# Dense identity products on TensorE ahead of twelve fronts and between the scores of the first heads' fill, with scores two steps less ahead

## The reference

```python
s0A: q = x @ W_q; latent = (x @ W_k + x @ W_v) @ W_down_kv       # attention with decay
     scores = (q_h @ k_h.T) / sqrt(d) * exp(-0.01 * |t - t'|)    # 16 heads of 16
     out = softmax(scores) @ v_h, heads joined, @ W_o
s1M, s3M: out = sum over experts of gate * gelu(x[top_k] @ w1) @ w2   # 8 experts, expert choice
s2B: retention: scan over time of v, times q, layernorm, gate, @ Wo
s4C: attention with rotary q and k, mask of blocks, window and 4 global keys
s5F, s7F: out = gelu(x @ U1 @ V1) @ U2 @ V2                      # low rank, 1024 hidden
s6D: gated recurrence: short convolutions, scan, rms norm, gate, @ Wo
```

## Time and profile before

| | |
|---|---|
| median of 3 runs | 3270.99 us (3268.53 to 3271.0) |
| profiled execution | 3270.93 us, span 3269.2 us |
| mean granted clock of TensorE | 0.914 of full speed |
| TensorE (PE) busy | 2802.9 us, 86% |
| VectorE (DVE), ScalarE (ACT), GpSimd (POOL) busy | 60%, 48%, 31% |

### The profile page before, as it was taken

How to read it: one execution, slowest core, us unless ns; L and a number is a source line. 1 busy time by engine, 2 the same in 40 slices (tenths; PEclk the granted TensorE clock), 3 DMA queues, 4 the chain that set the end, 5 groups by cost and what they waited for, 6 DMA issues and landing times. The chain is left out here.

```text
span 3269.2 us, 48231 instructions
## 1 busy us (share of the span) xinstructions
PE 2802.9 (86%) x15883; PEld 1690.3 (52%) x15883; DVE 1958.6 (60%) x4266; ACT 1558.7 (48%) x2949; POOL 1004.0 (31%) x1384
## 2 busy tenths in 40 slices
PE   6599999999986299997883499996969997888879
PEld 3244444444443198985551498983534443534443
DVE  6578878888826744443558644444956663527852
ACT  3347777777751145453111345442326665245544
POOL 3322222222201145452001245442664442120112
PEclk9779999999998599998996699997979998898879
DMA  7813232323224144432003244423243442200001
GB/s 254 282 46 83 66 86 67 85 67 80 62 70 134 45 91 86 95 71 65 0 0 130 65 96 84 98 38 89 79 123 96 101 99 66 56 1 0 0 7 46
DMA packets 183271, 253.89 MB, mean 78 GB/s; under 512 B 39416, under 2 KB 124152, under 8 KB 183056
## 3 DMA queue, kind: packets, MB, share of 16 engines
q1 hardware_dynamic: 151616, 216.89, 22.3%
q0 software_dynamic: 30720, 33.98, 6.5%
q10 hardware_dynamic: 720, 0.33, 0.1%
HBM read 156.53 MB, written 93.00 MB: 76 GB/s over the span
## 5 line engine op out<-in xcount | busy, mean ns | idle before, releaser
L2000 DVE CUSTOM_DVE_ANT_0 s0Ah_SD<-s0Ah_ps_s,s0Ah_table 128x1024 f32<-128x1024 f32 x512 | 607.1, 1223 | 157.1 <-PE s0Ah_ps_s L2055 157.1
L2024 ACT ACTIVATE s0Ah_PM<-s0Ah_ps_x 128x512 f32<-128x512 f32 x1024 | 530.1, 601 | 188.0 <-PE s0Ah_ps_x L2080 98.1
L2055 PE MATMUL s0Ah_ps_s<-s0Ah_plus_k,s0Ah_plus_q 48*128 48x512 f32 x1024 | 422.9, 477 | 31.9 <-DMA s0Ah_minus_k<-s0Ah_ones 28.0
L1980 POOL TENSOR_TENSOR s0Ah_DG<-s0Ah_SD,s0Ah_mx 128x128 f32<-128x128 f32 x512 | 205.5, 401 | 554.0 <-DVE s0Ah_mx L2000 554.0
L2055 PEld LDWEIGHTS s0Ah_ps_s<-s0Ah_plus_k,s0Ah_plus_q 48*128 48x128 f32 x1024 | 167.4, 193 | 279.6 <-DVE s0Ah_mx L2000 176.7
L2100 PE MATMUL s0Ah_ps_v<-s0Ah_PM,s0A_V 128*17 128x512 f32 x2048 | 271.9, 603 | 0.0
L2080 PE MATMUL s0Ah_ps_x<-s0Ah_plus_q,s0Ah_plus_k 50*128 50x512 f32 (+3 forms) x640 | 238.0, 389 | 0.0
L2260 DVE CUSTOM_DVE_ANT_0 s4Ch_SD<-s4Ch_ps_s,s4Ch_table 128x264 f32<-128x264 f32 x448 | 177.4, 431 | 94.6 <-PE s4Ch_ps_s L2345 90.1
L2080 PE MATMUL s0Ah_ps_x<-s0Ah_minus_q,s0Ah_minus_k 50*128 50x512 f32 (+3 forms) x640 | 218.9, 390 | 0.0
L2289 ACT ACTIVATE s4Ch_PM<-s4Ch_ps_x 128x512 f32<-128x512 f32 (+1 forms) x256 | 131.4, 564 | 113.7 <-PE s4Ch_ps_x L2372 110.5
L2089 PE MATMUL s0Ah_ps_x<-top_ident,s0Ah_DG 128*128 128x128 f32 x512 | 169.0, 330 | 0.0
(11 more groups left out here) (438 smaller groups left out, 6736.3 us busy)
## 6 DMA issues: line engine op xcount, KB each, us to landing
s0A_parts<-s0Ap_sp_top SPq DMA_DIRECT2D x32, 512.0 KB
s0A_parts<-s0Ap_sp_rest SPq DMA_DIRECT2D x32, 512.0 KB
s1W_raw_w<-in_L_ffn_w SPq DMA_DIRECT2D x16, 1024.0 KB
s3W_raw_w<-in_L_ffn_w SPq DMA_DIRECT2D x16, 1024.0 KB
s0Ah_plus_q<-s0A_parts SPq DMA_DIRECT2D x64, 128.0 KB, 2.5
s0Ah_plus_k<-s0A_parts SPq DMA_DIRECT2D x64, 128.0 KB, 3.0
s0Ah_minus_q<-s0A_parts SPq DMA_DIRECT2D x64, 128.0 KB, 3.0
s0Ah_minus_k<-s0A_parts SPq DMA_DIRECT2D x64, 128.0 KB, 3.2
```

The lines of the kernel that those rows point to most:

```text
L1980: nc.gpsimd.tensor_tensor(DG[p % 3][:, r * TB + t, :], SD[i % NSD][:, t * P:(t + 1) * P], mx[p % 3][:, r * TB + t:r * TB + t + 1].to_broad ...
L2000: nc.vector.tensor_tensor_reduce(SD[i % NSD][:, :], ps_s[i % 2][:, :, :].rearrange("p a n -> p (a n)"), table[:, (TB - 1 - t) * P:(TB - 1 ...
L2024: nc.scalar.activation(PM[n % NPB][:, :], ps_x[u % NX][:, :], ACT.Exp).then_inc(e_ok, 1)
L2055: x = nc.tensor.matmul(ps_s[i % 2][:, half, :], q[at(r), t * P:(t + 1) * P], k[at(r), half * GT:(half + 1) * GT], start=True, stop=True)
```

## The change

A new helper issues n matmuls of the identity (128 x 128) with the identity repeated four times (128 x 512) into a bank. It waits for nothing, signals nothing, and nobody reads its results; the bank is one whose first real use comes later on the same engine.

It is called first in TensorE's program of eight functions: `low_rank_ffn` (5 products), `retention` (7), `gated_recurrence` (5), `route` (6), `experts` (8, ahead of the first transposes), `project_rotary` (5), `heads_window` (6) and `project_heads` (8). As `low_rank_ffn`, `route`, `experts` and `project_heads` run twice, that makes 77 products in twelve phases. In the fill of `heads_decay` one product follows each score step from 19 on (9 products). AHEAD goes from U + 14 to U + 12, and TURN with it from 12 to 10.

```diff
@@ -155,6 +155,14 @@
             turn(b * 2 + h, h, True, True)
     turn(NG - 2, 0, True, False)
     turn(NG - 1, 1, False, False)
+
+
+def keep_dense(nc, ident, bank, n):
+
+
+    for _ in range(n):
+        nc.tensor.matmul(bank, ident[:, :], ident[:, :].unsqueeze(1).to_broadcast([P, GT // P, P]),
+                         start=True, stop=True)
 
 
 class FfnWeights:
@@ -382,6 +390,7 @@
                     at = (2 * k + j) * P
                     x = nc.tensor.matmul(ps_o[:, j * D:(j + 1) * D], QT[:, at:at + P], v2[:, :], start=True, stop=True)
                 x.then_inc(o_mm, 1)
+            keep_dense(nc, ident, ps_o[:, :], 5)
             pe.wait_ge(W.weights, W.loaded)
             turned(0, 0)
             turned(0, 1)
@@ -573,6 +582,7 @@
 
         @block.tensor
         def _(pe):
+            keep_dense(nc, ident, ps_m[:, :], 7)
             pe.wait_ge(raw.next_in, 16 * 4)
             pe.wait_ge(consts, START + 1)
 
@@ -817,6 +827,7 @@
 
         @block.tensor
         def _(pe):
+            keep_dense(nc, ident, ps_i[:, 0, :], 5)
             pe.wait_ge(W.weights, W.loaded)
             pe.wait_ge(consts, START + 1)
 
@@ -1059,6 +1070,7 @@
 
         @block.tensor
         def _(pe):
+            keep_dense(nc, ident, ps_p[:, :], 6)
             pe.wait_ge(weights, 48)
             def score(g):
                 pe.wait_ge(ln.hTok, START + (g + 1) * DC)
@@ -1343,6 +1355,7 @@
                                                      stop=(m == M - 1 and k % 2 == 1 and n == 2))
                             if m == M - 1 and k % 2:
                                 x.then_inc(o_mm, 1)
+            keep_dense(nc, ident, ps_o[:, 0, :], 8)
             transposes(0, 0, 0)
             expert_turns(pe, turn)
 
@@ -1833,6 +1846,7 @@
 
         @block.tensor
         def _(pe):
+            keep_dense(nc, ident, ps_r[:, 0, :], 5)
             ln.tensor(pe, 0)
             pe.wait_ge(raw.next_in, 16 * 3)
             pe.wait_ge(consts, START + 2)
@@ -1864,7 +1878,7 @@
 
     NP = B * H // 2
     U = 2 * TB
-    AHEAD = U + 14
+    AHEAD = U + 12
     TURN = AHEAD - U - 2
     NPB, NSD, NX = 12, 3, 3
     plus = [[ph.sb(f"plus_{n}{i}", [P, T], F32R) for n in "qk"] for i in range(4)]
@@ -2106,6 +2120,8 @@
                     score(i, half)
                 if i == U + 2:
                     turned(0)
+                if i > U + 2:
+                    keep_dense(nc, ident, ps_x[NX - 1][:, :], 1)
             for i in range(N):
                 ahead = i + AHEAD
                 if (i + TURN) % U == 0 and (i + TURN) // U < NP:
@@ -2413,6 +2429,7 @@
                 if t == TB - 1:
                     x.then_inc(pv_mm, 1)
 
+            keep_dense(nc, ident, ps_x[0][:, :], 6)
             pe.wait_ge(sign_ok, START + 1)
             for m in range(3):
                 x = nc.tensor.transpose(ps_x[NX - 1][:, m * P:(m + 1) * P], signs[:, m, :], ident[:, :])
@@ -2531,6 +2548,7 @@
 
         @block.tensor
         def _(pe):
+            keep_dense(nc, ident, ps_o[0][:, :, :].rearrange("p a n -> p (a n)"), 8)
             pe.wait_ge(weights, 16 * 2 * DC)
             pe.wait_ge(pick_ok, START + NG * DC)
             pe.wait_ge(top_ok, START + 1)
```

## The result

The changed kernel takes 3279.8 us (median of 20 executions, 3264.6 to 3284.4) against 3271.0 before (20 executions, 3266.5 to 3274.4). The ratio is 1.002, with a 95% interval of 1.0011 to 1.0029: about 0.2% slower, where the prediction said 3254.5 us and a range of 3245 to 3263.5. The 20 executions stand in two groups, nine from 3264.6 to 3274.9 and eleven from 3279.5 to 3284.4. The profiled execution (3271.4 us, span 3269.6) is of the lower group, so what its profile shows stands for that group and not for the median.

What follows compares the result with a forecast made beforehand. VectorE bounds the heads' fill, TensorE the steady loop, which starts at half clock. Heads -6.4, project_heads -3.4, experts -3.2, FFNs -2.4, rotary -0.7, route -0.4 sum to -16.5 us: 3270.93 to 3254.5, range 3245 to 3263.5.

Steps and rivals of the forecast that it cites:

- The failed step: Heads' fill: clock rises 4.4 us after 175.9, at 180.3; two steps cold, seven warm, fill ends at 190.6.
- -8.4 + 1.8 + 0.2 = -6.4 us: Heads: steady loop at full clock from its start -8.4, longer fill +1.8, two more steps carrying scores at loop's end +0.2.
- third rival: Heads' fill: its products do not raise the clock, loop begins cold; +12.3 us in place of -6.4, total 3273; chance 0.07.
- first rival: Fronts: the clock holds everywhere, so fronts taken at half give all; 3246 us or a little less; chance 0.10.
- TURN: Heads' steady loop: turned maxima of each later pair move from step 4 to 6; cost 0, 2 us to spare.
- fourth rival: Heads' steady loop: maxima come late, TensorE stands at 31 pair starts, 1 us each, total 3285; chance 0.04.
- The fronts: Waits ahead of stages: project_heads -3.4 us, experts -3.2, FFNs -2.4, rotary -0.7, route -0.4; window heads, retention, recurrence 0.
- second rival: Fronts: clock falls behind transposes; FFNs and route 0, experts -0.95 each, rotary +1; -9.3 us in all, 3261.6; chance 0.15.

Runs made afterwards that it cites:

- e3_ahead28: Kernel before with only AHEAD = U + 12 and TURN 10, no products anywhere: 3271.9 us, ratio 0.9999.
- e1_fronts: Changed kernel without its products in the heads' fill, AHEAD back at U + 14, products in the twelve fronts: 3259.9 us, ratio 0.9963.
- e4_burst4: e1_fronts plus four products in one row between the heads' fill and the steady loop: 3261.8 us, ratio 0.9968.
- e7_less2: e1_fronts without the products of heads_window and retention: 3260.2 us, ratio 0.996.
- e9_less2_burst3: e7_less2 plus three products in one row between the heads' fill and the steady loop: 3256.0 us, ratio 0.9961.

## Why the prediction was wrong, point by point

**The failed step** is this one: "The clock rises, by the mean delay, at 175.9 + 4.4 = 180.3: two steps cold, the other seven warm". The 4.4 us came from fronts where real matmuls on 128 rows stand back to back or nearly so. In the fill they stand alone between pairs of score matmuls on 48 rows, 2.0 us of each 3.15, and there the clock never rose, in any of the five profiles of fills with single products. The row that speaks against it was in the prediction: 45.76 us of 50 busy at 0.50. I read it as scores alone, but its last 11.2 us are the loop; the fill has 34.54 busy us of 38.37 (same columns, kernel before):

```profile
150.41:188.78 38.37, 34.54 (x62) 0.50 0.33 78
```

That says the same. I gave it a rival's chance of 0.07, when of the two kinds of work in a step one was known to raise the clock and the other known not to; that was no better than even.

Its terms: I had -8.4 + 1.8 + 0.2 = -6.4 us for the place; it was +16.6. The fill is 14.2 us longer (203.00 against 188.78) where I had 1.8, since nine steps took 3.15 each, and not two at 2.9 and seven at 1.5. The gain of 8.4 did not come, and the loop was cold for 25.3 us instead of 20.2, which cost about 2. The third rival had the mechanism right and gave +12.3 for it, 3273 in all; a cold step was 0.25 us dearer than I had it, and the loop's cold stretch longer. The range ended at 3263.5 because that case was left outside it.

Place and fronts together explain the profiled execution: 23.0 us more than forecast in the heads, 5.9 less behind them, 3271.4 in place of 3254.5. They do not explain the median, which lies 8.4 us higher; that part stays open with the two groups. Two sums were slightly off, with no effect: -16.5 from 3270.93 is 3254.4, and the first rival's terms give 3246.5 and not "3246 or a little less".

**TURN** was right: no wait for the copies at a pair's start, and e3_ahead28 at 0.9999. The fourth rival is out.

**The fronts** were right in kind and on the low side. Against my -10.1 us they gave -16.0 in the profiled pair and -12 (7 to 17) in e1_fronts. project_heads: -2.0 and -2.1, forecast -1.7 each. Experts: -2.3 and -0.8, forecast -1.6. FFNs: -2.1 and -1.6, forecast -1.2. Route -0.6 and -0.3, forecast -0.2 each. Rotary: -2.0 here, but -0.4 to -0.9 in most other profiles with its products, forecast -0.7. Recurrence: -3.0, forecast 0, and anything from -0.1 to -3.3 in the others. Retention and window heads, forecast 0, took up to 1 and about 2 us.

**The second rival** (the clock falls behind transposes) is right for one of the four fronts looked at here and in part for another; I had set it as one rule for all. In the FFN of stage 5 the clock was full through 3.2 us of transposes and waits, and the first projections took 1.98 us; in the experts of stage 1 likewise. In the last FFN it fell 3.2 us behind the last product and the same projections took 3.61 us, and in the experts of stage 3 it fell 5.0 us behind, 1.1 us into the projections; the gain there was 0.8 us against 2.3. The Trainium skill's statement ("TensorE: Matmul & The Clock Gate", "Part 4: PE-mode transpose") that transposes do not count as busy is not contradicted by either outcome. What does not follow from it is that products ahead of transposes are wasted: a clock that was up outlasted such a gap in three of these four places, if in the third only by that 1.1 us.

**The first rival**, full clock at all fronts, fell as well. Beyond my forecast it wanted -2.0 us in the experts, -3.0 in the FFNs, -0.9 in the rotary front and -2 in the window heads, -7.9 in all; the profile has +0.1, -1.3, -1.3 and 0, -2.5 in all. The rest of the 5.9 us by which the fronts gave more than forecast came from the recurrence (-3.0), project_heads (-0.7) and route (-0.5), less retention's +0.8. At the recurrence the clock was still up from the phase before when the products began at 2942.80, and stayed up for 9.35 us more, where in the kernel before it had fallen 3.2 us ahead of the first transposes. I had put this front at 0 because I took the clock as fallen by then. As the other profiles have anything from -0.1 to -3.3 us there, the full 3.0 is in part luck.

## What to carry to other kernels

Work that is put in to raise the clock is better issued in rows than one piece at a time. In this kernel single products between scores on 48 of the array's 128 rows never raised it, while rows of two (in the second of them), three and four did, though behind rows of three it also fell again. Before spending them, look in the trace whether the work between them holds the clock by itself (here 34.5 busy us of 38.4 at half clock said no). At fronts where TensorE waits for something else anyway such products are nearly free and gave some 12 us of 3271. With transposes and short waits behind, the clock lasted to the real work at some fronts and not at others; at the window heads and retention, where I expected nothing, they gave nothing. Versions with the fronts and without single products in the fill (e1_fronts, e4_burst4, e7_less2, e9_less2_burst3: 3256 to 3262 us, ratios 0.996 to 0.997) beat both kernels; between these four the runs can't tell.

## What the runs showed of the hardware that I had not expected

A TensorE that is busy without a gap can stay at half clock for long. The steady loop of the heads, the same instructions each time, was cold at its start for 14.0 us in one profile, and for 19.1 to 35.4 us in the nine others of kernels that begin it cold; once up it stayed up for the remaining 740 us or so. Behind a row of three products the same loop lost the clock again after 3.4 us and stayed cold for 20.5. Such swings, 10 us and more in the length of a cold stretch, are as large as most edits of this kind, so that one profile of each kernel does not price them: the profiled pair of this case differs by 0.5 us and the medians by 8.8.
